# A decoder layer in fp32 on one core: first norm by tile, the last tiles' chains ordered by tile, and a new order of the closing sums

## The reference

```python
x = x + attn(layernorm(x), w_q, w_k, w_v, w_o)        # 32 heads, 8 kv heads, head dim 128, causal
x = x + xattn(ctx, ctx, layernorm(x))                  # scores ctx x query, softmax, context
x = x + ffn(layernorm(x), gate, up, down)              # 4-bit weights, inner width 1376, output to fp16
# layernorm(x) = (x - mean) / sqrt(var + 1e-5), without weights
# ffn: inter = silu(x @ Wg) * (x @ Wu); out = (inter @ Wd).astype(float16)
```

## Time and profile before

| | us |
|---|---|
| median of 3 runs | 763.44 (761.32 to 765.03) |
| the profiled execution | 763.18 |
| its span, first to last instruction | 761.4 |
| TensorE busy (matmuls) | 739.5 (97%) |
| VectorE busy | 507.7 (67%) |
| ScalarE busy | 382.9 (50%) |
| GpSimd busy | 307.3 (40%) |
| mean granted clock of TensorE | 0.994 |

### The profile page before, as it was taken

How to read it: one execution, slowest core, us unless ns; L and a number is a source line. 1 busy time by engine, 2 the same in 40 slices (tenths; PEclk the granted TensorE clock), 3 DMA queues, 4 the chain that set the end, 5 groups by cost and what they waited for, 6 DMA issues and landing times.

```text
span 761.4 us, 11217 instructions
## 1 busy us (share of the span) xinstructions
PE 739.5 (97%) x3732; PEld 618.0 (81%) x3732; DVE 507.7 (67%) x669; ACT 382.9 (50%) x961; POOL 307.3 (40%) x334
## 2 busy tenths in 40 slices
PE   8999999999999999999999999999999979999995
PEld 7888888888888888888888888888887747888873
DVE  6457736763675477457736773676358867988897
ACT  3365526453553554265526453553556655556553
POOL 4352314322321332152304322422244543698895
PEclk9999999999999999999999999999999999999999
DMA  9412033202322040213023101302720002122002
GB/s 298 118 56 80 1 107 110 79 37 69 114 75 82 25 162 17 96 28 141 0 86 110 59 28 39 110 28 77 251 74 2 1 0 56 45 80 77 28 11 111
DMA packets 44352, 56.44 MB, mean 74 GB/s; under 512 B 7433, under 2 KB 26057, under 8 KB 44329
## 3 DMA queue, kind: packets, MB, share of 16 engines
q1 hardware_dynamic: 44328, 56.15, 23.0%
HBM read 45.26 MB, written 10.88 MB: 74 GB/s over the span
## 4 chain that ended last, share of the span: by engine, by line
PE 89%; DVE 4%; POOL 2%; issue 2%; ACT 2%; POOLq 0%; ACTq 0%
PE psum L443 20%; PE psum L445 20%; PE psum L444 20%; PE psum L559 7%; PE psum L618 5%; PE psum L619 5%; PE psum L568 3%; PE psum L641 2%; PE psum L640 2%; DVE stats L1081 1%; PE psum L463 1%; PE psum L449 1%; PE psum L470 1%; ACT probs L809 1%; POOL o_sum L1041 1%
## 5 line engine op out<-in xcount | busy, mean ns | idle before, releaser
L993 POOL TENSOR_TENSOR probs<-probs,rowinv 128x512 f32<-128x512 f32 x64 | 71.1, 1111 | 307.9 <-DVE rowinv L1226 307.9
L809 ACT ACTIVATE probs<-probs,negmax 128x128 f32<-128x128 f32 x256 | 99.8, 391 | 60.6 <-DVE negmax L1213 60.6
L443 PE MATMUL psum<-xt_hi,wq_hi 128*128 128x512 f32 x256 | 104.4, 408 | 0.0
L802 ACT CAST pt_hi<-psum 128x512 fp32r<-128x512 f32 x64 | 37.5, 586 | 128.3 <-PE psum L568 128.3
L443 PE MATMUL psum<-wo_hi,at_hi 128*128 128x512 f32 x256 | 100.2, 391 | 0.5 <-DVE at_lo L1244 0.5
L445 PE MATMUL psum<-xt_hi,wq_lo 128*128 128x512 f32 x256 | 100.2, 391 | 0.0
L444 PE MATMUL psum<-xt_lo,wq_hi 128*128 128x512 f32 x256 | 99.9, 390 | 0.0
L445 PE MATMUL psum<-wo_hi,at_lo 128*128 128x512 f32 x256 | 99.7, 389 | 0.0
L444 PE MATMUL psum<-wo_lo,at_hi 128*128 128x512 f32 x256 | 99.6, 389 | 0.0
L1244 DVE TENSOR_TENSOR at_lo<-psum,at_hi 128x512 fp32r<-128x512 f32 x64 | 44.1, 689 | 71.9 <-ACT at_hi L836 71.9
L721 ACT ACTIVATE qt<-psum 128x512 f32<-128x512 f32 x64 | 38.0, 594 | 75.8 <-PE psum L445 74.1
(11 more groups left out here) (133 smaller groups left out, 1630.4 us busy)
## 6 DMA issues: line engine op xcount, KB each, us to landing
wq_raw<-in_L_attn_w_q SPq DMA_DIRECT2D x8, 1024.0 KB, 5.5
wo_raw<-in_L_attn_w_o SPq DMA_DIRECT2D x8, 1024.0 KB, 7.8
unpacked_w<-u_q SPq DMA_DIRECT2D x8, 688.0 KB, 3.0
gw<-unpacked_w SPq DMA_DIRECT2D x20, 256.0 KB, 3.5
unpacked_w<-u_q SPq DMA_DIRECT2D x6, 512.0 KB, 2.6
u_q<-in_L_ffn_gate_qweight SPq DMA_DIRECT2D x8, 344.0 KB, 7.2
u_q<-in_L_ffn_up_qweight SPq DMA_DIRECT2D x8, 344.0 KB, 3.9
u_q<-in_L_ffn_down_qweight SPq DMA_DIRECT2D x10, 256.0 KB, 3.3
```

Of the source, the lines that this page charges most:

```text
L443: pe.matmul(dst, a_hi, b_hi, start=start, stop=False)
L809: e = act.activation(probs[:, t % 2, j, :], probs[:, t % 2, j, :], ACT.Exp, bias=negmax[:, t % 2, j:j + 1], accum_out=rowsum[:, t % 2, j:j ...
L993: pool.tensor_tensor(probs[:, t % 2], probs[:, t % 2], rowinv[:, t % 2, :].unsqueeze(2).to_broadcast([P, HG, P]), ALU.mult).then_inc(prob_ ...
```

## The change

In the first norm, tiles 0 to 3 go singly: VectorE adds epsilon, GpSimd does only the power, VectorE the Newton step in two operations and, for tiles 0 to 2, a bias, with which ScalarE norms; tile 3 is normed by VectorE. The four tiles are turned into four banks. VectorE copies the high part of tile 3 itself; the low parts follow it. GpSimd's weight splits wait for the norm of tile 3. The first projection does its four high x high matmuls ahead of the others. There are 10 fillers at first, and none behind tile 2. Tiles 4 to 7 have a GpSimd chain each.

In every single-tile chain of GpSimd the Newton step takes two operations, and -0.5 (var + eps) is made ahead.

In the last group, the tenth slot and the four rounds are replaced by a list for each engine, ordered by tile. In slot 8 tile 6's count goes behind the low part of tile 7's heads. The scales are converted in slot 4 (the fifth) instead of behind the loop. The third turns of tiles 5 and 7 use another bank.

At the end VectorE adds tiles 0, 1 and 3 between the first and the last two sums of the second half, and `Y_POOL` is (2, 5).

```diff
-    DEVIATIONS = [(0, 2), (2, 2), (4, 2), (6, 2)]
-    WARM_FIRST, WARM_NEXT = 14, 3
+    FIRST_ACT = 3
+    FIRST_PAIRS = [(0, 2), (2, 2)]
+    WARM_FIRST, WARM_NEXT = 10, 3
...
+        LATE = BH + 1
...
+        def third_bank(b):
+            return BK_XT if b >= LATE and b % 2 else BK_FT
...
-        Y_POOL = (1, 4, 6)
+        Y_POOL = (2, 5)
...
+        FIRST_TURN = (BK_T, BK_VT, BK_PV, BK_O, BK_T, BK_VT, BK_T, BK_VT)
...
             def turn_first(b):
+                if b < FIRST_ACT:
+                    pe.wait_ge(first_normed, b + 1)
+                else:
+                    pe.wait_ge(ln_ready[0], b - FIRST_ACT + 1)
+                if b >= BH:
+                    pe.wait_ge(ln_lo[0], b - BH + 1 if b < BH + 2 else b - 1)
+                turn_tile(FIRST_TURN[b], xn[:, b % 2, :]).then_inc(ln_turned[0], 1)
+            def project_first(unit, bank):
+
+                hi, lo = weight(unit)
+                cols = slice(0, HALF)
+                pe.wait_ge(w_hi, 1)
+                pe.wait_ge(ln_hi[0], BH - 1)
+                pe.wait_ge(first_hi, 1)
+                for c in range(HC):
+                    pe.matmul(psum[:, bank, :], hi[:, c, :], xt_hi[:, c, cols], start=(c == 0), stop=False)
+                pe.wait_ge(ln_lo[0], BH)
+                for c in range(HC):
+                    pe.matmul(psum[:, bank, :], hi[:, c, :], xt_lo[:, c, cols], start=False, stop=False)
+                pe.wait_ge(w_lo, 1)
+                for c in range(HC):
+                    mm = pe.matmul(psum[:, bank, :], lo[:, c, :], xt_hi[:, c, cols], start=False, stop=(c == HC - 1))
...
-            for t in range(SLOTS, ALL_SLOTS):
-                cross_scores(t)
...
+            out_heads(LAST, NB - 1)
+            cross_scores(5)
+            turn_queries(6)
+            turn_third(3)
+            cross_scores(6)
+            cross_output(5)
+            turn_queries(7)
+            cross_scores(7)
+            cross_output(6)
+            pe.wait_ge(ln_lo[2], BH)
...
+            first_half(0, 0)
+            first_half(1, 0)
+            cross_output(7)
+            turn_third(4)
+            first_half(2, 0)
+            turn_third(5)
+            first_half(3, 0)
+            first_half(4, 0)
+            turn_third(6)
+            first_half(5, 0)
+            first_half(6, 0)
+            turn_third(7)
+            first_half(7, 0)
...
+            first_norm(0)
+            first_norm(1)
+            first_tile(0)
+            first_tile(1)
+            first_unit(0)
+            first_norm(2)
+            first_tile(2)
...
+            third_norm(3)
+            second_norm(6)
+            queries_out(6)
+            cross_exp(5)
+            third(3)
+            second_norm(7)
+            cross_exp(6)
+            queries_out(7)
+            third_norm(4)
+            cross_exp(7)
+            act.wait_ge(scales_ready, 3)
+            first_first(0, 0)
+            third_norm(5)
+            third(4)
+            first_first(1, 0)
+            third_norm(6)
+            third(5)
+            third_norm(7)
+            third(6)
+            third(7)
...
+                pool.tensor_scalar(n, meanvar[:, b, 1:2], EPS, -0.5, ALU.add, ALU.mult).then_inc(rstd_step, 1)
                 after(pool.tensor_scalar(v, meanvar[:, b, 1:2], EPS, 1.0, ALU.add, ALU.mult))
                 after(pool.tensor_tensor(r, v, halfneg[:], ALU.pow))
-                after(pool.tensor_tensor(n, r, r, ALU.mult))
-                after(pool.tensor_tensor(n, n, v, ALU.mult))
-                after(pool.tensor_scalar(n, n, -0.5, 1.5, ALU.mult, ALU.add))
-                after(pool.tensor_tensor(r, r, n, ALU.mult))
+                after(pool.tensor_scalar(n, n, r, r, ALU.mult, ALU.mult))
+                after(pool.tensor_scalar(r, n, 1.5, r, ALU.add, ALU.mult))
...
+            for b in range(BH):
+                first_pow(b)
+            pool.wait_ge(ln_ready[0], BH - FIRST_ACT)
             split_second(HBLK[0], 1)
             split_second(HBLK[1], 2)
+            for i in range(BH):
+                first_deviation(BH + i)
+                split_second(HBLK[2 + i], 3 + i)
...
+            inverse_deviation(7, 1)
+            for b in range(4, NB):
+                inverse_deviation(b, 2)
...
+            first_count(0)
+            first_epsilon(0)
+            first_count(1)
+            first_epsilon(1)
+            first_half_variances(0)
+            first_deviation(0)
+            first_bias(0)
+            first_deviation(1)
+            first_bias(1)
...
+            first_deviation(3)
+            first_norm(3)
+            dve.wait_ge(ln_turned[0], BH)
+            dve.tensor_copy(xt_hi[:, :, (BH - 1) * P:HALF],
+                            psum[:, FIRST_TURN[BH - 1], :].rearrange("p (c t) -> p c t", c=HC)).then_inc(first_hi, 1)
+            first_second(0)
+            for b in range(1, BH):
+                first_second(b)
...
+            cross_add(4)
+            cross_count(4)
+            add_heads(LAST, NB - 1)
+            heads_count(LAST, NB - 1)
+            cross_max(5)
+            cross_inverse(5)
+            third_second(3)
+            cross_max(6)
+            cross_inverse(6)
+            cross_add(5)
+            cross_count(5)
+            cross_max(7)
+            cross_add(6)
+            cross_inverse(7)
+            cross_count(6)
+            cross_add(7)
+            cross_count(7)
+            third_second(4)
             dve.wait_ge(scales_ready, 3)
+            first_add(1, 0, 0)
+            first_add(1, 1, 0)
+            third_second(5)
+            third_second(6)
+            third_second(7)
+            first_add(2, 0, 0)
+            first_add(2, 1, 0)
+            first_add(3, 0, 0)
+            first_add(3, 1, 0)
...
-            last_sums(0)
-            last_sums(1)
+            last_sums(0, (1, 2, 3))
+            last_sums(1, (1,))
             last_adds(0)
+            last_sums(1, (2, 3))
             last_adds(1)
```

More of the change, by code:

```diff
@@ L481, in _ @@
                 turn_first(b)
-                warm(WARM_NEXT)
-            pe.wait_ge(ln_lo[0], BH)
-            for i in range(FIRST_BLOCKS):
+                if b != BH // 2:
+                    warm(WARM_NEXT)
+            project_first(HBLK[0], BK_PROJ[0])
+            for i in range(1, FIRST_BLOCKS):
                 pe.wait_ge(w_lo, i + 1)
@@ L745, in first_tile, with first_norm @@
             def first_tile(b):
-                tile_first(b, 0, xt_hi, (BK_T, BK_VT)[b % 2])
-            for b in range(BH):
-                first_tile(b)
-                first_unit(b)
+                tile_first(b, 0, xt_hi, FIRST_TURN[b])
+            def first_norm(b):
+                act.wait_ge(first_shift, b + 1)
+                if b >= 2:
+                    act.wait_ge(ln_turned[0], b - 1)
+                act.activation(xn[:, b % 2, :], xacc[:, b, :], ACT.Identity, bias=shift[:, b:b + 1],
+                               scale=rstd[:, b:b + 1]).then_inc(first_normed, 1)
+            first_norm(0)
[5 more added lines that the diff above has]
+            first_tile(2)
+            for i in range(1, BH):
+                first_unit(i)
             for i in range(FIRST_BLOCKS):
@@ L787, in queries_out, with third @@
                             SCALE).then_inc(ln_hi[1], 1)
-            def third(t):
-                b = t - AT_NORM3
+            def third(b):
                 if 0 <= b < NB:
-                    tile_first(b, 2, ft_hi, BK_FT)
+                    tile_first(b, 2, ft_hi, third_bank(b))
             def group(g, more):
                 step, blocks = g * NB, g * NBLK + FIRST_BLOCKS
-                for t in range(SLOTS):
+                for t in range(SLOTS if more else SLOTS - 1):
                     if 1 <= t <= NB:
@@ L804, in group @@
                     if not more:
[L805 removed]
+                        third_norm(t - AT_NORM3)
                     if t < NB:
@@ L1016, in _ @@
             group(LAST, False)
-            for t in range(SLOTS, ALL_SLOTS):
-                cross(t)
+            inverse_deviation(7, 1)
+            for b in range(4, NB):
+                inverse_deviation(b, 2)
             def inner(n):
@@ L1198, in cross_last, with cross_count, heads_count, scales @@
                                       ALU.add).then_inc(x_added, 1)
+            def cross_count(b):
+                if 0 <= b < NB:
                     dve.wait_ge(x_added, b + 1)
                     count(b, 2)
+            def heads_count(g, u):
+                dve.wait_ge(o_added, g * NB + u + 1 + PRIME)
+                count(u, 1)
+            def scales():
+                dve.wait_ge(ld_s, 16 * 3)
+                dve.tensor_copy(gu_s[:], gu_s16[:]).then_inc(scales_ready, 1)
+                dve.tensor_copy(d_s[:], d_s16[:]).then_inc(scales_ready, 1)
+                dve.tensor_copy(ident16[:], ident[:]).then_inc(scales_ready, 1)
             def group(g, more):
                 step = g * NB
```

(2 more changed lines are left out.)

223 lines of the change are left out of this document (104 added, 119 removed).

## The result

The changed kernel takes 761.48 us (median of 20 runs, from 760.06) against 762.95 (760.87 to 765.03, 20 runs) before: a ratio of 0.9978, 95% interval 0.9968 to 0.9988. That is 1.5 us less where 4.15 were forecast. Its profiled execution took 761.72 us, with a span of 759.9. Eighteen of its 20 times lie in two heaps, 760.1 to 760.4 (eight) and 761.4 to 762.0 (ten); the others are 764.17 and one run of 1244.51 at a mean granted clock of 0.557, which the ratio leaves out.

A forecast was written before the change was run, and what follows sets the result against it. TensorE was taken as full except in holes at the start, the last tiles and the end; -0.95 - 3.9 + 0.7 = -4.15 took 763.18 to 759.0 and the median 763.44 to 759.3, range 757.2 to 762.2.

The forecast's parts named there:

- What bounds the kernel: Whole kernel: TensorE is full in the long inner stretches, so gains ahead of one arrive at its end.
- nothing: Inner stretches where TensorE is full: nothing in the change touches them.
- Part 1: First norm, tiles handled singly: fifth k matmul at 15.03, a gain of 0.95 us.
- Part 2: Slots 3 to 8: GpSimd's single-tile chain falls from 2.29 to 2.15 us, moving the tail up 0.15 to 0.2.
- Part 3: Last tiles, ordered by tile: second half of the first feed-forward tile starts at 625.2, not 629.13, 3.9 us earlier.
- rival A: Last tiles: the clock still falls there, costing 1.4 and 0.5 us, 1.7 for both, giving 761.0; chance 0.14.
- Part 4: Closing sums, adds and stores: a loss of 0.7 us, bounds a gain of 0.4 to a loss of 1.2.
- B: End: it loses nothing, as early stores leave sooner and the rest overlap better, giving 758.6; chance 0.12.
- C: Start: clock rises late, halving the gain (759.8, chance 0.08), or stays low (766.5, 0.04); chance 0.12 together.
- D: Last tiles: the order brings less than half, a supposedly hidden step being in tile 7's chain, giving 761.5; chance 0.10.
- The sum: Whole kernel: -0.95 - 3.9 + 0.7 = -4.15 us, taking the median from 763.44 to 759.3.

The follow-up runs named there:

- e5: Kernel before with only the new order of the last tiles, start and end as before: 759.64 us against 762.72, ratio 0.9969.
- e2: Kernel before with only the new end: 762.82 us against 762.52, ratio 1.0009.
- e6: Kernel before with 21 filler matmuls in the holes of the last tiles, order untouched: 761.89 us against 762.72, ratio 0.9995.
- e7: Changed kernel with 10 filler matmuls between the closing turns of tiles 0 to 3 and 4 to 7: 759.71 us, ratio 0.9970 to the kernel before.
- e10: Changed kernel unaltered, measured again as control: 760.08 us against 762.73 for the kernel before, ratio 0.9974.
- e9: Changed kernel with one 64-column matmul ahead of each of the 10 later feed-forward blocks: 760.98 us, ratio 0.9985 to the kernel before.
- e3: Kernel before with only the new first norm: 761.68 us against 762.52, ratio 0.9990.

## Why the prediction was wrong, step by step

**What bounds the kernel.** Held. The stretches of the earlier trace rows kept PE full (516.00 of 516.00 and 60.00 of 60.00), and what was won ahead of them arrived behind them. What failed is the word "nothing": the inner stretch is not the same length in each execution.

**Part 1, start.** Forecast 0.95, measured 0.7 (34.35 to 33.67). The mechanism held, the four early matmuls gained nothing. What is missing is small terms in a row. The turn of tile 2 starts at 10.96 for 10.85, and the copy of tile 3's high part at 12.09 for 11.9; from there to the fifth matmul, 0.19 late, all goes as reckoned. (A Newton step's two operations take 0.27 and 0.21 us on VectorE, where I had set 0.18 for every small one. That brings tile 3's own norm from 10.5 to 10.97, but it ends as PE begins to turn tile 2, and costs nothing.) The v projection starts 0.74 earlier than before (17.17 for 17.91), the loop only 0.63. The rest goes at tile 7:

```profile
28.00 1.50 DVE L1164 TENSOR_SCALAR xn<-xacc,meanvar,rstd 128x512 f32<-128x512 f32 x1 [1.23 <-POOL rstd L1032]
...
29.56 0.66 PE L460 MATMUL psum<-ident,xn 128*128 128x128 f32 x4
```

Its scale stands behind GpSimd's splits and chains, its norm runs beside a split and ends at 29.50, and PE turns it at 29.56. I had feared such a thing for tile 4, at 0.3; it came at tile 7, at some 0.1. Whether the added wait of GpSimd or the chains in place of pairs made it late is not separated. The splits themselves (from 11.05) were never waited for.

**Part 2, slots 3 to 8.** Forecast 0.15 to 0.2, measured nothing: from the loop to the first query turn e5 needs 532.07 us and before 532.09. Two operations less on GpSimd, but the new forms cost more. The groups of the changed kernel from 604 to 631 us: busy us, mean ns.

```profile
L1018 POOL TENSOR_SCALAR newton<-newton,rstd 128x1 f32<-128x1 f32 x7 | 2.4, 344 | 0.8
L1019 POOL TENSOR_SCALAR rstd<-newton,rstd 128x1 f32<-128x1 f32 x7 | 1.9, 267 | 0.7
```

With the first operation's 0.28 of queue time the chain is 2.28 long, before 2.29. I had taken 2.15, between bounds of 2.0 and 2.3.

**Part 3, tail.** The walk through the new order was good: Silu foretold at 631.8 in the time frame of before, 631.91 in e5; ten adds without a gap, 625.25 to 631.9 in the changed kernel. But tile 7's last chain was 0.8 late (626.01 for 625.2). Half of that is a queue I forgot, GpSimd's chain of tile 6:

```profile
620.43 0.26 POOL L985 TENSOR_SCALAR shift<-meanvar,rstd 128x1 f32<-128x1 f32 x1
...
620.77 0.19 POOL L980 TENSOR_SCALAR newton<-meanvar 128x1 f32<-128x1 f32 x1
```

In e5 tile 7's count ends at 620.36 (0.4 later than foretold, the other half), tile 6's chain at 620.69, and tile 7's begins at 620.77. The 0.8 went through to the adds, which in e5 run from 625.87 to 632.5 and were foretold for 625.1 to 631.7. That the Silu is only 0.1 late is luck: I had put it behind the tenth add, and it starts behind the ninth.

```profile
631.14 0.74 DVE L1297 SCALAR_TENSOR_TENSOR f_g<-psum,gu_s,f_g 128x512 f32<-128x512 f32 x1
...
631.91 1.06 ACT L942 ACTIVATE f_g<-f_g 128x1024 f32<-128x1024 f32 x1 [2.58 <-DVE f_g L1297]
```

The failing step is the other side of the subtraction. I took 635.57 for the place of the Silu before, from an execution whose clock had fallen twice, although were among my rows and I even priced a fall in rival A. Without falls it is at 633.3 (e2, e6), so the order brings 1.5 us and not 3.9, and the rest is the insurance against falls. How much of that a median gets depends on how many executions of before have them: e6 puts it at 0.8 us (its interval includes none at all), where I had booked 2.1. I then attached the result to the median of three runs (763.44), with more runs 762.5 to 762.95.

**Part 4, end.** Forecast a loss of 0.7, measured 1.2, just above my bound. The order of events came as foretold up to the last sums (6.24 us behind the first closing sum, foretold 6.18). Then 0.4 was lost to the clock. In each of the five traces with this end and no fillers it fell 3.0 to 4.9 us behind the first closing sum, ahead of the pause or in it (3.7 to 6.3), and the late turns ran at 0.50. Without the fall (e7) the loss is 0.8, close to the 0.7. I had written that PE turns tiles 4 to 7 "from 755.7 instead of 753.56", that is a pause of more than 2 us, and had not applied to it what I had read from the 2.16 us of the earlier trace rows.

**The rivals.** A, a clock fall in the new tail, was in none of the eleven traces with it. The rule of the Trainium skill that I had weighed ("TensorE: Matmul & The Clock Gate", section "A second HAM failure mode: psum-queue depth-cycling") was thus not borne out: pauses of 0.2 to 0.9 us between groups left the clock up. B fell (the end loses). C came in one trace of ten, at 1.4 us. D, half of the tail, has the right number (761.5) by luck: a step in tile 7's chain was late, as it said, but by 0.8 us, and the rest is the base, the end and the spacing.

**The sum.** Between the two profiled executions it closes: start -0.63, tail -3.64 (with the falls of before), spacing +1.57, end +1.23 make -1.47, and the spans are 761.4 and 759.9. In this pair the tail's term nearly came, and of the 2.7 that are missing 1.6 are the spacing, put at nothing, 0.5 the end, 0.3 the start and 0.3 the tail. Over many executions the tail's gain lies between: the ratio of e5 gives 2.4, with an interval of 1.5 to 3.2, and no closer. By milestones, against an undisturbed execution of before (761.0): start -0.7, tail -1.5, end +1.2 make 760.0, and the changed kernel's lower heap is at 760.1 to 760.4, in e10 at 759.6 to 760.2. The median of 761.48 lies 1.3 above it, since half of the runs lie in the upper heap, as the profiled one with its long spacing does; of the others only the time is known. The median of before lies 1.5 to 1.9 above its own 761.0, by falls and, it seems, spacing. The difference of two such medians is 1.5 in one comparison and 2.65 in another, and neither is the 4.15 of a sum against one disturbed trace.

## What to carry to other kernels

Ahead of a subtraction, ask whether the trace of before is an undisturbed one. A clock fall in a hole that the change fills belongs to the gain only as often as executions have it, and the lowest of the runs says what is left without it (761.0 here, where the trace said 763.18). Each new pause of TensorE is to be checked against the pauses by which the clock fell in the same trace. And where stores leave in a fixed order, the one that is ready last belongs last: that alone was worth 0.8 us here, more than the start.

## What had not been expected of the hardware

- TensorE at a granted clock of 1.00, never waiting, follows matmul on matmul (128x512) by 0.2289 us in eleven traces and by 0.2333 in four, from 641 to 645 us on to the end of the network, on several chips and for one and the same kernel. In the four every step between 660 and 680 us is 0.233 or 0.234; in the others, e9 with its extra matmuls aside, they go between 0.225 and 0.233. From 100 to 530 us all fifteen traces have a mean step of 0.2279. The cause is open. It moves the kernel by 1.2 to 1.6 us, about as much as the change itself.
- The clock's falls are not a function of the program alone. Of three traces with the old tail and no fillers in it, the kernel before had two falls there, e3 one (from 628.9 us), and e2 none, with the same matmuls and much the same waits (in front of tile 7's query turn 2.16, 2.15 and 2.15 us).
- Small operations differ by form: with two pointers 0.34 us on GpSimd, with one 0.27, without 0.19; on VectorE 0.27, 0.21 and 0.15.
